# Single-head stage of a graph network: kept adjacency exponentials, and the row of ratios spread by one product of high and low rows

## The reference

```python
# stages A and B: a transformer layer with 8 heads and the adjacency in its weights, then its feed-forward part
# stages C (W1, 8 heads) and D (W2, 1 head):
def graph_attention(x, bias, W, a_src, a_dst):        # bias is the adjacency
    h = jnp.einsum('bnd,dhk->bhnk', x, W.reshape(D, H, Dh))
    s = jnp.einsum('bhnk,hk->bhn', h, a_src)
    t = jnp.einsum('bhnk,hk->bhn', h, a_dst)
    e = jax.nn.leaky_relu(s[:, :, :, None] + t[:, :, None, :], 0.2)
    attn = jax.nn.softmax(e + bias[:, None, :, :], axis=-1)
    return jnp.einsum('bhij,bhjk->bhik', attn, h)
attn = graph_attention(layer_norm(x, g1, b1), adj, W1, a_src1, a_dst1) + x
out  = graph_attention(layer_norm(attn, g2, b2), adj, W2, a_src2, a_dst2) + attn
```

## Time and profile before

| what | value |
|---|---|
| median of 3 runs | 1324.27 us (1323.82 to 1328.11) |
| profiled execution: its own time, span | 1329.56 us, 1327.8 us |
| mean granted TensorE clock in it | 0.963 |
| PE busy | 1178.1 us (89%) |
| DVE busy | 903.8 us (68%) |
| ACT busy | 645.1 us (49%) |
| POOL busy | 424.2 us (32%) |
| adjacency loads over the whole kernel | 48 of 256 KB |

### The profile page before, as it was taken

How to read it: one execution, slowest core, us unless ns; L and a number is a source line. 1 busy time by engine, 2 the same in 40 slices (tenths; PEclk the granted TensorE clock), 3 DMA queues, 4 the chain that set the end, 5 groups by cost and what they waited for, 6 DMA issues and landing times.

```text
span 1327.8 us, 40299 instructions
## 1 busy us (share of the span) xinstructions
PE 1178.1 (89%) x15340; PEld 990.7 (75%) x15340; DVE 903.8 (68%) x2466; ACT 645.1 (49%) x1495; POOL 424.2 (32%) x641
## 2 busy tenths in 40 slices
PE   6688889888889879999999999988888888799998
PEld 5577777677777768999989899866666666577776
DVE  6666666566666665445354454569999999879997
ACT  1566665665666645445363544623333323245553
POOL 2512111111111102213122231226556665554442
PEclk9799999999999999999999999998888889989999
DMA  7100110000010000000000000000000000013222
GB/s 207 40 27 27 37 40 26 27 26 27 27 34 10 10 2 1 1 1 0 0 0 0 0 0 0 1 18 18 17 16 8 16 16 17 12 38 89 71 88 79
DMA packets 50192, 35.50 MB, mean 27 GB/s; under 512 B 5536, under 2 KB 49824, under 8 KB 50080
## 3 DMA queue, kind: packets, MB, share of 16 engines
q1 hardware_dynamic: 45184, 33.04, 8.3%
q10 hardware_dynamic: 4896, 0.80, 0.5%
HBM read 25.44 MB, written 8.39 MB: 25 GB/s over the span
## 4 chain that ended last, share of the span: by engine, by line
PE 59%; DVE 19%; issue 12%; POOL 4%; ACT 4%; DVEq 1%; ACTq 1%; POOLq 0%; DMA 0%
DVE pp L583 5%; PE BK L1261 5%; PE BK L1259 5%; PE BK L1260 5%; PE BK L1052 4%; PE BK L1054 4%; PE BK L1053 4%; PE BK L1176 4%; PE BK L1150 4%; PE F L1077 2%; PE BK L1143 2%; POOL x_all L770 2%; PE F L1068 2%; PE F L1052 2%; PE F L1069 2%
## 5 line engine op out<-in xcount | busy, mean ns | idle before, releaser
L793 POOL TENSOR_TENSOR ve<-mv,eps_l 128x4 f32<-128x4 f32 x64 | 13.0, 204 | 525.4 <-DVE mv L268 525.4
L982 ACT ACTIVATE gf<-BK,bcol 128x512 f32<-128x512 f32 x128 | 88.3, 690 | 187.7 <-PE BK L1054 175.1
L404 DVE TENSOR_TENSOR pt_sb<-BK,ft 128x512 f32<-128x512 f32 x128 | 85.5, 689 | 119.7 <-PE BK L1150 119.5
L901 ACT ACTIVATE e_sb<-BK,nmx 128x128 f32<-128x128 f32 x512 | 140.7, 386 | 28.5 <-DVE nmx L398 28.5
L1259 PE MATMUL BK<-wf_hi,gh 128*128 128x256 f32 x512 | 145.4, 284 | 0.0
L1261 PE MATMUL BK<-wf_lo,gh 128*128 128x256 f32 x512 | 144.1, 282 | 0.0
L1260 PE MATMUL BK<-wf_hi,gl 128*128 128x256 f32 x512 | 144.0, 281 | 0.0
L583 DVE SCALAR_TENSOR_TENSOR pp<-BK,bqs,gt 128x128 f32<-128x128 f32 x512 | 139.0, 336 | 1.6 <-PE BK L1331 0.8
L490 DVE TENSOR_TENSOR gl<-gf,gh 128x512 fp32r<-128x512 f32 x128 | 92.0, 718 | 67.5 <-ACT gh L983 65.5
L504 DVE TENSOR_TENSOR x_all<-BK,x_all 128x256 f32 (+1 forms) x64 | 27.2, 425 | 125.5 <-PE BK L1261 125.5
L263 DVE BATCH_NORM_STATS2 st<-x_all 128x6 f32 (+1 forms) x256 | 96.0, 413 | 10.7 <-DMA x_all<-in_x_dram 7.7
(11 more groups left out here) (180 smaller groups left out, 3078.3 us busy)
## 6 DMA issues: line engine op xcount, KB each, us to landing
adj_in<-in_adj_dram SPq DMA_DIRECT2D x48, 256.0 KB, 2.9
x_all<-in_x_dram SPq DMA_DIRECT2D x16, 512.0 KB, 4.4
out_dram<-y SPq DMA_DIRECT2D x16, 512.0 KB, 3.2
s_wf<-in_L_gnn_Wf_dram SPq DMA_DIRECT2D x2, 1024.0 KB, 12.0
s_w<-in_L_gnn_W_dram SPq DMA_DIRECT2D x2, 256.0 KB, 8.5
s_wq<-in_L_gnn_Wq_dram SPq DMA_DIRECT2D x1, 256.0 KB, 3.6
s_wk<-in_L_gnn_Wk_dram SPq DMA_DIRECT2D x1, 256.0 KB, 4.2
s_wv<-in_L_gnn_Wv_dram SPq DMA_DIRECT2D x1, 256.0 KB, 4.6
```

The source lines that it names most:

```text
L901: e = act.activation(e_sb[:, j, :], LE[:, r, q, :], ACT.Exp, bias=nmx[:, j:j + 1], scale=1.0)
```

## The change

The exponentials of all 64 adjacency graphs get a buffer of their own, `gt_all` (32 KB in each partition, laid over the feed-forward weights of stage B). Stage C writes it and stage D reads it. In stage D the loads, the transposes and the exponentials of the adjacency fall away. `sel_d` falls away, and the row of ratios is spread as in stage C: ACT takes the exponential of `u_sb` a second time, into `rp`, POOL writes the low rows, and PE makes one float32r product. ACT's first exponential of a chunk waits for POOL's low rows of the chunk before (in place of PE's spreading product), and the second for the spreading two chunks before.

```diff
+                at_wf1 = (nc.sbuf_base + 31) // 32 * 32
-        sel_d = sb("sel_d", [P, P])
+        gt_all = overlay(at_wf1, at_wf1 + 4 * KT * FF * 4)("gt_all", [P, NG * P])
-        gt_sb = [o(f"gt{r}", [P, G, P]) for r in range(2)]
+        def gts(i, g):
+            return gt_all[:, bass.ds((i * G + g) * P, P)]
-                done(dve.tensor_copy(sel_d[:], ident[:, 0:1].to_broadcast([P, P])))
...
-                                                 scalar=bq_sb[par][:, g, 16 + h:17 + h], in1=gt_sb[par][:, g, :],
+                                                 scalar=bq_sb[par][:, g, 16 + h:17 + h], in1=gts(i, g),
...
             def d_scale(i, par):
                 dve.wait_ge(d_bc, i + 1)
-                dve.wait_ge(c_gt, i + NC + 1)
...
-                                             scalar=bq_sb[par][:, g, 16:17], in1=gt_sb[par][:, g, :],
+                                             scalar=bq_sb[par][:, g, 16:17], in1=gts(i, g),
...
             def c2_step(i, half, par):          # SP
-                if not (isinstance(i, int) and i == NC - 1):
-                    load_c(i + 1, 1 - par, CD)
...
-            load_c(0, 0, CD)
...
+                    if first == CD:             # POOL, at the end of norms
+                        pool.wait_ge(d_xb, (i + 1) * G)
+                        rows_lo(i + NC, par)
...
-                act.wait_ge(adj_t, c - NC + 1)
-                act.activation(gt_sb[par][:].rearrange("p g n -> p (g n)"), F[0][:], ACT.Exp).then_inc(c_gt, 1)
                 if first == CC:
+                    act.wait_ge(adj_t, c - NC + 1)
+                    act.activation(gt_all[:, bass.ds(i * W4, W4)], F[0][:], ACT.Exp).then_inc(c_gt, 1)
...
                     act.wait_ge(c_rows, (i + NC) * 5 + 5)
-                    if isinstance(i, int) and i == 0:
-                        act.wait_ge(c_lo, NC)
-                    else:
-                        act.wait_ge(d_bc, i)
+                    act.wait_ge(c_lo, i + NC)
                     act.activation(rb[0:ROWS, :], u_sb[:], ACT.Exp).then_inc(c_rb, 1)
+                    wait_for(act, d_bc, i - 1)
+                    act.activation(rp[par][0:ROWS, :], u_sb[:], ACT.Exp).then_inc(c_rp, 1)
                     normalise(i, CD, (0, 1, 2))
...
-            def d_bcast(i):
-                pe.wait_ge(c_rb, i + NC + 1)
+            def d_bcast(i, par):
+                pe.wait_ge(c_rp, i + NC + 1)
+                pe.wait_ge(c_lo, i + NC + 1)
                 wait_for(pe, d_pp, i * G)
-                pe.matmul(BK[:, 0, :], sel_d[:], rb[:], start=True, stop=True).then_inc(d_bc, 1)
+                pe.matmul(BK[:, 0, :], sel[:, 0, :], rp[par][:], start=True, stop=True).then_inc(d_bc, 1)
...
                 if back:
-                    d_bcast(i - 1)
-                adj_turn(i + CD, half, par, CD)
+                    d_bcast(i - 1, 1 - par)
```

More of the change, by code:

```diff
@@ L79, in build @@
         eps_l1 = sb("eps_l1", [P, G])
-        whl = {}
+        whl, at_wf1 = {}, 0
         for name, kt, n in (("wq", KT, D), ("wk", KT, D), ("wv", KT, D), ("wf1", KT, FF),
                             ("wf2", FT, D), ("w1", KT, D), ("w2", KT, D), ("wst1", KT, P), ("wst2", KT, P)):
+            if name == "wf1":
+                at_wf1 = (nc.sbuf_base + 31) // 32 * 32
             whl[name] = [sb(f"{name}_{part}", [P, kt, n], F32R) for part in ("hi", "lo")]
@@ L1125, in adj_turn @@
             def adj_turn(c, half, par, first):
-                before = {CA: 0, CC: NC // 2, CD: NC}[first]
+                before = {CA: 0, CC: NC // 2}[first]
                 pe.wait_ge(adj_ld[par], (half + 1 + before) * 16)
@@ L1397, in _ @@
             chunks(pe, c2_step)
-            d_bcast(NC - 1)
+            d_bcast(NC - 1, last)
             for g in range(G):
```

## The result

| kernel | median | ratio to before, 95% interval | a chunk of stage D |
|---|---|---|---|
| changed, first measurement | 1334.53 us (before 1325.44, 7 runs each) | 1.0065 (1.0042 to 1.0087) | 10.23 us |
| changed, second measurement (k1) | 1333.98 us (before 1326.98) | 1.0051 (1.0032 to 1.0070) | 10.23 us |

The kernel got slower, by some 7 to 9 us, under 1%, and both intervals lie clear of 1. The last column is the distance of two starts of the exponential `rb` on ACT, in the profiled execution. Before the change it was 9.81, and 9.82 as the mean of 13 chunks.

The account below looks back on a forecast made before the run. A loop through several engines was taken to bound stage D: 0.50 us in each of chunks 1 to 13 (6.5), plus 0.1, 0.2 and 0.5, made 7.3 us on 1324.27, thus 1331.6 us, range 1324.5 to 1341.

Parts of the forecast that it names:

- What goes lies beside the loop: Stage D's removed adjacency loads, transposes and exponentials: claimed hidden, apart from 0.11 us a chunk on the six products.
- the loop: Stage D chain from `rb` through normalisation, transposes, `xh`, `xl`, six products and maxima to next `rb`; sets the 9.81 us chunk.
- The block of the small copy: DVE's L533 in stage D stands still while POOL's `rows_lo` runs: about 0.9 us instead of 0.17, L634 0.66 later.
- Slack ahead of `xl`: DVE's idle time between its statistics and `xl` in stage D: 0.07 us, so `xl` starts 0.61 later.
- The gain of 0.11 on the six products: PE in stage D: first product, 0.50 us against 0.39, no longer queues behind adjacency transposes; 0.11 us a chunk gained.
- The chunk: Length of one stage D chunk: 0.50 us more, to 10.3 us, with the maxima starting later.
- ACT's second exponential is swallowed by the block: ACT in stage D: normalisation L921 starts 0.16 us later, hidden by DVE's longer delay ahead of `xl`.
- The clock falls too: Rival: 1.8 us of PE idle ahead of stage D's six products lowers its clock; 1335 to 1344 us, chance 0.27.
- PE is the bound: Rival: PE's busy time in stage D is real work, so removing some gains up to 8.7 us, 1315.6; chance 0.05.

Follow-up runs that it names:

- k3: Kernel before with only the adjacency exponentials kept for stage D; old spreading, no second exponential, no `rows_lo`: 1326.83 us, ratio 0.9996.
- k4: Changed kernel with one more wait: in stage D POOL's `rows_lo` starts only after the small copy: 1331.83 us, ratio 1.0036.
- k6: Kernel before plus one unneeded POOL subtraction of `rows_lo`'s shape in each chunk of stage D: 1333.63 us, ratio 1.0056.
- k2: Changed kernel with the small copy of stage D reading PSUM instead of SBUF: 1331.06 us, ratio 1.0027.
- k7: Against k3: stage D's rows made in F[0], first three of the six products started after the first half of `xl`: 1327.18 us, ratio 0.9998.
- k9: Against k3: ACT also takes the second exponential of `u_sb` into `rp`, which nobody reads: 1329.40 us, ratio 1.0032.
- k10: Against k7: two of four weights moved behind the exponents, statistics wait and one reciprocal moved later, W2 products earlier: 1318.63 us, ratio 0.9948.

## Why the prediction was right

The forecast was 7.3 us more, 1331.6, within 1324.5 to 1341. Measured were 1334.53 and 1333.98, 9.1 and 7.0 us above the kernel before in the same series; the profiles place 6.3 us of it.

- *What goes lies beside the loop.* Right: k3 has the chunk and the time of before.
- *The block of the small copy.* Right in place and kind: 0.87 us measured, about 0.9 forecast, and L637 at +2.46 us instead of +2.52. k4 and k6 show it as an effect of the overlap: the one removes it without removing work, the other makes it with an instruction that shares no data. That the cause is a port that both engines use is the Trainium skill's account ("SBUF — State Buffer", "Who interferes with whom"). All rows here agree with it, the copies out of PSUM in k2 too; no run looks at a port.
- *Slack ahead of `xl`.* Mis-sized: 0.07 was taken from the end of the statistics to the start of `xl`. Where its inputs are ready, L285 starts before the recorded end of the instruction ahead (L285 at 1244.84, L268 until 1244.93), so the true slack was larger than the gap in the rows. The shift was 0.42 us instead of 0.61, so the slack had been about 0.16 to 0.18. (0.66 less 0.07 would have been 0.59; the 0.61 is a slip.)
- *The gain of 0.11 on the six products.* Wrong: the first still lasts 0.50 us after 1.58 us of idle. That is not a queue behind the transposes. And k7 shows that the products were not what the maxima waited for: the forecast let these start 0.02 us after the statistics (1246.39 and 1246.41), where the kernels before and after both have 0.12 to 0.13.
- *The chunk.* +0.41 us as a mean, against +0.50 forecast. The path is the forecast one, but part of the nearness is luck: the slack mis-sized by 0.11 and the gain of 0.11 that didn't come cancel, and what is left is mostly the block, 0.60 instead of 0.66. The stage: +6.3 us against +7.3.
- *ACT's second exponential is swallowed by the block.* Right: 0.16 forecast; k9 has 0.15 alone, and in the changed kernel the block covers it. Hence taking the block away gives back 0.25 and not 0.42.
- *The clock falls too.* Not in the chunks that were counted: each has about 1.58 us of idle (and 0.19 ahead of the transposes), against 1.8 forecast, at a granted clock of 1.00 from 1180 to 1312 in both profiles of the changed kernel. The prediction sorted the cases by the length of one idle time (1.64 and 1.97 us), and that doesn't hold up. In k3 PE idles 2.39 us at the place of the 1.97 (until 1170.91), and the clock stays at 1.00 from 1168 to 1180. In k1's first chunk it falls to 0.50 right behind an idle time of 1.34 us, with 1.21 and 0.71 us of idle a little earlier. And the 1.97 us themselves came little more than 1 us after a stretch at 0.50 (until 1167.2). Which idle times lower the clock stays open here; that the prediction gave a fall 0.27 and none came in the counted chunks doesn't show that its sorting was right.
- *PE is the bound.* Refuted by k3: with the adjacency transposes gone the chunk still takes 9.83 us.

## What to carry to other kernels

A GpSimd instruction can lengthen a VectorE copy that has nothing to do with it. So for each instruction that is added to GpSimd, look at which copies within SBUF VectorE starts while it runs; the rows here show it for copies of 128x4 and 128x32. Look at the duration of each against its usual one, since the standstill counts as busy time. Then take the copy's source from PSUM, or order the two by a wait. Work that was removed beside the loop was worth nothing by itself; what it gave is a free buffer that lets the order on the loop be changed (k3, then k10). In a loop with two paths that are nearly even, removing work from one shows nothing: k7 had to be followed by k10.

## What was not expected of the hardware

- The first of a run of float32r products lasts 0.50 us and the later ones 0.39, whether transposes stand right ahead of it or an idle time of 1.58 us.
- A wait of VectorE for its own last two statistics: 0.13 us from their end to the next start (k7, 1244.20 to 1244.33). With that wait behind the maxima it is 0.04 (k10, 1248.08 to 1248.12), though there the products end only at 1248.02 and may set the start as well.
